# A graph-network stack on one core: a seam piece one slot later, the last round's normalisation behind the relu, clearing and small loads in other slots

## What is computed

```python
x = layernorm(x + prelu(adj @ (x @ W0) + b0))            # layer 0
x = layernorm(x + adj @ (x @ W1) + b1)                   # layer 1
h = x                                                    # layer 2: five rounds of a gated unit
for l in range(5):
    m = A.T @ (h @ Wg[l])            # A = (adj != 0)
    r = sigmoid(m @ Wir + h @ Whr); z = sigmoid(m @ Wiz + h @ Whz)
    n = tanh(m @ Win + r * (h @ Whn)); h = (1 - z) * n + z * h      # biases left out
x = layernorm(x + h * mask)
for g, idx in enumerate(GROUPS):                         # layer 3: only nodes 0..24, five node groups
    a = D^-1/2 (adj[idx][:, idx] + I) D^-1/2
    fused[idx] += w[g] * relu(a @ relu(a @ x[idx] @ W1g + b1g) @ W2g + b2g)
x = layernorm(x + fused)
```

## Time and profile before

| what | value |
|---|---|
| median of 3 runs | 989.18 us (988.3 to 990.01) |
| the profiled execution | 988.7 us, span 986.9 us |
| PE busy | 950.6 us, 96% |
| DVE busy | 820.8 us, 83% |
| ACT busy | 770.9 us, 78% |
| POOL busy | 749.0 us, 76% |
| stage one, 0 to 163 us | PE busy 151.1 us |
| middle stage, 163 to 872 us | PE busy 705.1 of 709 us |
| closing stage, 872 to 987 us | PE busy 94.5 of 115 us |

### The profile page before, as it was taken

How to read it: one execution, slowest core, us unless ns; L and a number is a source line. 1 busy time by engine, 2 the same in 40 slices (tenths; PEclk the granted TensorE clock), 3 DMA queues, 4 the chain that set the end, 5 groups by cost and what they waited for, 6 DMA issues and landing times.

```text
span 986.9 us, 19418 instructions
## 1 busy us (share of the span) xinstructions
PE 950.6 (96%) x6010; PEld 574.5 (58%) x6010; DVE 820.8 (83%) x2077; ACT 770.9 (78%) x1324; POOL 749.0 (76%) x844
## 2 busy tenths in 40 slices
PE   7999998999999999999999999999999999989894
PEld 6999996554444544444554555554445455468783
DVE  5999998898879999988898899789879987946555
ACT  5698896888887877887887889788887977865552
POOL 4777888567989897987988798889778887974101
PEclk9999999999999999999999999999999999999997
DMA  7543450333744563375448345654943563440020
GB/s 191 132 119 108 131 129 18 63 72 65 118 75 65 102 115 81 59 133 105 81 80 154 76 66 115 115 107 89 164 88 55 108 127 67 77 91 18 26 66 28
DMA packets 295406, 90.74 MB, mean 92 GB/s; under 512 B 222514, under 2 KB 295175, under 8 KB 295303
## 3 DMA queue, kind: packets, MB, share of 16 engines
q1 hardware_dynamic: 295302, 89.49, 45.8%
HBM read 28.67 MB, written 8.81 MB: 38 GB/s over the span
## 4 chain that ended last, share of the span: by engine, by line
PE 71%; DVE 10%; POOL 6%; issue 6%; ACT 3%; DMA 2%; SPq 0%; POOLq 0%; DVEq 0%; ACTq 0%
PE psum L1560 16%; PE psum L1565 16%; PE psum L1561 16%; PE psum L1485 8%; PE psum L1592 6%; POOL shared L765 2%; PE psum L1640 2%; PE psum L1673 2%; DMA shared<-shared 1%; DVE x3q L1020 1%; PE psum L1659 1%; PE psum L1483 1%; DVE shared L1342 1%; PE psum L1518 1%; DVE shared L1349 1%
## 5 line engine op out<-in xcount | busy, mean ns | idle before, releaser
L765 POOL TENSOR_TENSOR shared<-shared 128x512 f32<-128x512 f32 x160 | 203.7, 1273 | 34.6 <-ACT shared L974 34.5
L724 POOL TENSOR_TENSOR shared<-shared 128x512 f16<-128x512 f32 x128 | 148.3, 1158 | 52.9 <-ACT shared L928 52.8
L1565 PE MATMUL psum<-shared,wx_hi 128*128 128x512 f16 x480 | 182.1, 379 | 2.0 <-DVE shared L1368 1.7
L1560 PE MATMUL psum<-shared,wh_hi 128*128 128x512 f16 x480 | 182.2, 380 | 0.5 <-DVE shared L1342 0.4
L1560 PE MATMUL psum<-shared,wx_hi 128*128 128x512 f16 x480 | 181.9, 379 | 0.0
L1561 PE MATMUL psum<-shared,wx_lo 128*128 128x512 f16 x480 | 181.9, 379 | 0.0
L1565 PE MATMUL psum<-shared,wh_hi 128*128 128x512 f16 x480 | 181.9, 379 | 0.0
L1561 PE MATMUL psum<-shared,wh_lo 128*128 128x512 f16 x480 | 181.9, 379 | 0.0
L1342 DVE SCALAR_TENSOR_TENSOR shared<-psum,bhn,shared 128x512 f32<-128x512 f32 x160 | 119.9, 749 | 52.4 <-ACT shared L945 49.9
L974 ACT ACTIVATE shared<-psum,brz,unscale 128x512 f32<-128x512 f32 x160 | 124.2, 776 | 46.2 <-PE psum L1565 46.1
L910 ACT ACTIVATE shared<-psum 128x512 f16<-128x512 f32 x160 | 95.6, 597 | 52.7 <-PE psum L1592 52.7
(11 more groups left out here) (183 smaller groups left out, 1742.8 us busy)
## 6 DMA issues: line engine op xcount, KB each, us to landing
m<-in_adj_dram SPq DMA_DIRECT2D x32, 256.0 KB, 3.0
m<-in_x_dram SPq DMA_DIRECT2D x32, 256.0 KB, 3.4
adjr<-in_adj_dram SPq DMA_DIRECT2D x32, 256.0 KB, 3.2
out_dram<-x SPq DMA_DIRECT2D x8, 768.0 KB
shared<-shared SPq DMA_TRANSPOSE x192, 3.2
out_dram<-shared SPq DMA_DIRECT2D x32, 50.0 KB
v<-in_L_gnn_W_dram SPq DMA_DIRECT2D x10, 128.0 KB, 2.4
x3q<-x SPq DMA_DIRECT2D x16, 50.0 KB
```

Of the source, the lines that this page charges most:

```text
L724: nc.gpsimd.tensor_tensor(HT_LO[s % 2], HT[s][:, :], HT_HI[s % 2], ALU.subtract).then_inc(b_htl, 1)
L765: nc.gpsimd.tensor_tensor(ZH[s % 2][:, :], ZW[s % 2][:, :], HT[s][:, :], ALU.mult).then_inc(b_zh, 1)
L1560: mm(dst, w_h[:, col:col + P], h[:, :], start=start, stop=False)
L1565: return mm(dst, w_h[:, col:col + P], lo[:, :], start=False, stop=stop)
```

## The change

**Seam.** For step 33 alone, `second_inner` moves from piece 1 to piece 2 and `transposed_y1` from piece 2 to piece 3, one slot later each.

**Closing stage.** `support_out(0)` goes to slot 162, ahead of the last tanh. HID, TT and TN get other addresses, so HID's first relu waits for the last state (`b_h`) where it waited for `b_fl`, and the copies wait for `b_fl`. `rest(k)` stands behind the relu of its step on ACT and DVE; on POOL it stays where it was. Its slots are no longer six a step but from 4, 10, 16, 18, 20 to 22.

**Clearing, loads and scaling.** Other slots for five of the sixteen clearings (45, 46, 65, 66 and 110 become 39, 59, 69, 79 and 99); small loads only in slots with t mod 20 outside 2 to 5; the last scaling of groups 3 and 4 in two slots.

Step sizes become a list, `IN_STEP`, which holds eight times sixteen as before; slices over graphs are written with its entry and come out the same.

In the places of tensors and the slots of `rest`:

```diff
-    REST = 6
+    REST_FROM = (4, 10, 16, 18, 20, LAST_LAG)
...
-        HID = [part([P, CS]) for c in range(HC)]
         TT = part([P, CS])
         TN = part([P, PAIRS * P])
+        assert used[0] <= RT_AT
+        used[0] = RT_AT
+        HID = [part([P, CS]) for c in range(HC)]
...
-                first = TURN + 4 + k * REST
-                for j in range(first, min(first + REST, TURN + LAST_LAG)):
+                for j in range(TURN + REST_FROM[min(k, 5)], TURN + REST_FROM[min(k + 1, 5)]):
```

On ACT:

```diff
-                if part == 2 and has(3):
+                if part == (3 if k == ALONE else 2) and has(3):
                     transposed_y1(k)
...
+                if t == ITEMS + 2:
+                    support_out(0)
...
-                    if gth(x) == GROUPS - 1:
-                        support_out(0)
...
+                if has(0):
+                    n = IN_STEP[k]
+                    act.wait_ge(c_h[0], k + 1)
+                    if k == 0:
+                        act.wait_ge(b_h, ITEMS)
...
+                    last.then_inc(c_rh[0], 1)
                 if k >= 1:
                     rest(k - 1)
...
                 if has(0):
-                    act.wait_ge(c_h[0], k + 1)
+                    n = IN_STEP[k]
+                    act.wait_ge(c_t, k + 1)
                     if k == 0:
                         act.wait_ge(b_fl, GROUPS)
```

On DVE:

```diff
-                if i in (17, 18, 19):
-                    for g in ((1,), (2,), (3, 4))[i - 17]:
+                if i in (17, 18, 19, 20):
+                    for g in ((1,), (2,), (3,), (4,))[i - 17]:
...
                 if has(3):
                     apply_q(k - 3)
-                if k >= 1:
-                    rest(k - 1)
...
                     last.then_inc(c_rh[1], 1)
+                if k >= 1:
+                    rest(k - 1)
```

On PE, and the tables of slots:

```diff
-                if part == 1 and has(3):
+                if part == (2 if k == ALONE else 1) and has(3):
                     second_inner(k)
...
-L3_DEG, L3_AN = 6, 21
-L3_AT = (3, 4, 8, 9, 13, 14, 32, 33, 44, 45, 46, 47, 48, 49, 52, 53, 64, 65, 66, 67)
+L3_DEG, L3_AN = 6, 22
+L3_AT = (3, 4, 8, 9, 13, 14, 32, 33, 44, 45, 46, 47, 48, 49, 52, 53, 64, 65, 66, 67, 68)
...
-ZERO_AT = (31, 45, 46, 50, 51, 65, 66, 70, 71, 85, 86, 90, 91, 105, 106, 110)
-M2_LOAD, M2_PER = 76, 1
+ZERO_AT = (31, 39, 50, 51, 59, 69, 70, 71, 79, 85, 86, 90, 91, 99, 105, 106)
+FREE_OF_STORES = [t for t in range(76, 160) if t % 20 not in (2, 3, 4, 5)]
+M2_AT = FREE_OF_STORES[:4 * sum(len(r) for r in RUNS)]
+N2_AT = FREE_OF_STORES[len(M2_AT):len(M2_AT) + 4 * NG]
...
-N2_LOAD, N2_PER = 118, 1
```

More of the change, by code:

```diff
@@ L58, in graph_stack_kernel @@
     BY_ACT = STEPS_A - 2
-    REST = 6
+    REST_FROM = (4, 10, 16, 18, 20, LAST_LAG)
     GC = 16
-    STEPS_C = B // GC
+    IN_STEP = [GC] * (B // GC)
+    FROM = [sum(IN_STEP[:k]) for k in range(len(IN_STEP))]
+    STEPS_C = len(IN_STEP)
     PAIRS = GC // 2
@@ L988, in step_c @@
                 if k >= 1:
                     rest(k - 1)
+                if has(1):
+                    n = IN_STEP[k - 1]
+                    act.wait_ge(c_o, k)
+                    ov = OT[:, :].rearrange("p (b s c) -> p b s c", b=2, c=NODES)[:, 0:by_bank(n), :, :]
+                    oa = OA[:, :].rearrange("p (b s c) -> p b s c", b=2, c=ADDED)[:, 0:by_bank(n), :, :]
+                    for g in range(NG):
+                        c = OFFS[g] - NODES
+                        nc.scalar.activation(oa[:, :, :, c:c + SIZES[g]] if g else ov, slots2(2, g, n), ACT.Relu,
+                                             bias=nwb2[:, g:g + 1], scale=nw[:, g:g + 1]).then_inc(c_ro, 1)
@@ L990, in step_c @@
                 if has(0):
-                    act.wait_ge(c_h[0], k + 1)
+                    n = IN_STEP[k]
+                    act.wait_ge(c_t, k + 1)
                     if k == 0:
                         act.wait_ge(b_fl, GROUPS)
-                    for g in range(NG):
-                        last = nc.scalar.activation(grp(HID[0], g), by_group(0, g), ACT.Relu,
-                                                    bias=b1T[:, g * HC:g * HC + 1])
-                    last.then_inc(c_rh[0], 1)
@@ L1006, in step_c @@
-                if has(0):
-                    act.wait_ge(c_t, k + 1)
                     for g in TT_ON_ACT:
-                        last = nc.scalar.activation(slots(TT[:, :], g), per_graph(by_group(4, g), g), ACT.Copy)
+                        last = nc.scalar.activation(slots(TT[:, :], g, n), per_graph(by_group(4, g, n), g), ACT.Copy)
                     last.then_inc(c_tt, 1)
@@ L1382, in apply_q @@
                 wait_apart(dve, c_rsq, k + 1)
-                for i in range(QUADS):
+                for i in range(IN_STEP[k] // G4):
                     last = nc.vector.tensor_scalar(xq[0:QN, i * D:(i + 1) * D], xq[0:QN, i * D:(i + 1) * D],
@@ L1425, in step_c @@
                     wait_apart(dve, c_bsq, k - 1)
-                    for i in range(QUADS):
+                    for i in range(IN_STEP[k - 2] // G4):
                         last = nc.vector.bn_aggr(MVQ[0:QN, 2 * i:2 * i + 2], STQ[0:QN, 6 * i:6 * i + 6])
@@ L1632, in step_c @@
                     pe.wait_ge(c_tts, k)
-                    for i in range(PAIRS):
+                    for i in range(IN_STEP[k - 1] // 2):
                         last = nc.tensor.transpose(psum[0:W2, 6 * 512 + i * P:6 * 512 + (i + 1) * P],
```

124 lines of the change are left out of this document (64 added, 60 removed).

## The result

The changed kernel takes 984.59 us (median of 6 runs, 984.18 to 985.43). The kernel before, run beside it, takes 989.63 (6 runs, 988.3 to 993.12). The ratio is 0.9943, with a 95% interval of 0.9924 to 0.9962. The profiled execution took 984.47 us around a span of 982.4, against 988.7 around 986.9. So it is 4.2 us faster from profile to profile (4.5 by the spans), 5.0 by the medians and 5.6 by the ratio, whose interval goes from 3.8 to 7.5 us. The forecast was 981.3, in a range of 978.5 to 985.5; the narrower band of 979.8 to 982.8, which it gave 60%, was missed.

A forecast was written before the change was run, and what follows sets the result against it. PE is busy 96% of the span, so gains come only where it stands: 1.34 + 0.90 + 1.82 + 0.94 + 2.43 = 7.4 us off the profiled 988.7 gives 981.3 us, range 978.5 to 985.5.

The forecast's parts named there:

- Rival 1: Closing stage, steps 2 and 3: the clock drops in PE's new waits, 1.4 us twice, so 984.1 us; chance 8%.
- seam: Start of the middle stage: PE's 2.60 us wait for POOL is filled until item 2's transpose lands; 1.34 us gained.
- pair in slots 67 and 68: Middle stage: two 36-element DVE operations go into two slots instead of both into slot 67; 0.9 us gained.
- stores, slots 86, 106, 126: Middle stage: without small loads around each store, the transposes behind the stores land in time; 1.8 us gained.
- clearings, slots 42, 62, 82, 102: Middle stage: five of sixteen clearings change slots, counted at nothing, 0.3 us either way.
- start of the closing stage: Support's evacuation ahead of the last tanh: PE leaves its wait sooner and the first relu starts earlier; 0.94 us gained.
- its steps: Closing stage, steps 1 to 5: 4.33 us excess of step 3 goes, 0.95 us comes back in steps 2 and 3; 2.43 gained.
- Rival 2: Stores: the small load is not what slows the transpose, so 1.3 to 1.8 us stay, about 983.0 us; chance 12%.
- rival 4: Slots 108 to 117: weight loads and small loads meet, transposes land late, 13.6 us over ten slots, 995 us; chance 3%.

## Why the prediction was partly right

Its time was 3.3 us too low, its range held the time, and its sign was right. That the range held it is in part luck: its upper end was there for the rivals, and none of them is what happened. Rival 1 had even named 984.1 us. But the clock stood at 1.00 from 884 to 944 us, and the two steps took the 12.51 us of the main forecast; the time alone would have pointed to the wrong cause. Term by term, against the profile of before:

| term | forecast, us | measured, us |
|---|---|---|
| seam | 1.34 | 1.27 |
| pair in slots 67 and 68 | 0.90 | 0.94 |
| stores, slots 86, 106, 126 | 1.82 | 1.50 |
| clearings, slots 42, 62, 82, 102 | 0 (0.3 either way) | -2.83 |
| start of the closing stage | 0.94 | 0.90 |
| its steps | 2.43 | 2.51 |
| all else | 0 | -0.1 |
| sum | 7.4 | 4.2 |

**The step that failed** is one sentence: "Five of the sixteen clearings change slots, three of them out of slots next to DVE's scalings; I count that at nothing, with 0.3 us either way." It looked at where the clearings left, not at what they came to stand before. The row was in the trace: POOL's gap of 0.34 us ahead of L735, for an operation of 0.81, and DVE's L1323 0.07 us ahead of it. Leaving slots 45, 46, 65 and 66 gave nothing: slots 46 and 66 stayed at 4.60 and 4.54 (4.58 and 4.53 before). The bound of 0.3 had no row under it. With -2.83 us in its place (of which slot 82's 0.42 is uncertain) the forecast would have been 984.1, against 984.47 in the profile and 984.59 by the median.

**The seam, the pair and the start** held with their mechanisms: item 2 was held by its transpose, one 36-element operation a slot costs 0.18 us, and L1006 is no longer released by POOL. The prediction's reading that the tiny operations wait for a turn is borne out: in the kernel after each takes 1.13 us (from 454.06 and from 458.57) and ends 0.05 us after POOL's L733, which began 0.08 us ahead of it.

**The stores** were mis-sized by 0.3. The transpose behind the store in slot 86 still took 4.9 us to land with the small load gone, and 3.9 in slot 106:

```profile
DMA to landing us min/median/max: 4.9/4.9/4.9
...
DMA to landing us min/median/max: 3.9/3.9/3.9
```

In eight other kernels with the loads moved slot 86 took 4.33 to 4.97 us, so up to 0.6 stays there with the store alone ahead of the transpose. Rival 2 was right in part. In slot 86 the row of the prediction held: 4.9 us is 0.26 over the 4.64 that are free, and the slot is 0.28 longer than 4.33. Of rival 4 (weight loads and small loads meet) nothing came: slots 110 to 118 are at 4.33 to 4.35.

**The closing steps** were right in sum, and each of the two waits was 1.1 us, inside the ends given. But the 4.33 us of excess that the sum starts from hold the fall of the clock, 1.5 to 1.7 us, which came in only two of five executions. Averaged over the profiles the steps are worth 1.5 us, 0.9 less than forecast, and the seam 2.2, 0.9 more. That the two terms cancel is luck. Rival 1, the clock falling in the new waits, was not seen in any of the six profiles that have them. But the argument against it was wrong: the 2.60 us wait brought the clock down in three of five executions, and the 1.72 us wait in one.

With these averages the places sum to 4.4 us (2.2 + 0.9 + 1.7 - 2.8 + 2.4), so they do not account for the 5.0 by the medians against 4.2 by the profiles; the interval of 3.8 to 7.5 holds both. The first profile of the kernel before was one of its better executions: 988.7, where its medians in four sets of runs are 989.6 to 990.4. The changed kernel has none of the waits of 2.60, 2.80 and 1.72 us, and its six runs lie within 1.3 us of each other; those of the kernel before beside it within 4.8.

## What to carry to other kernels

A small operation moved to an engine with idle time overall needs a gap of its own size where it lands. If there is none, see what it pushes, and what that then meets on the engine that shares a port with it. Ask the windows by slot, not the page's share (POOL is 76% busy in the span and 95% in those slots). And take two or three profiles of the kernel before when PE has long waits in it: behind the same wait the clock fell in some executions and not in others, so a term read from one of them may be a throw of a coin.

## What the runs showed of the hardware

- A POOL clearing of 0.81 us lengthens DVE's float32 scalings in SBUF (L1331) from 0.66 to 1.23 us, although it reads nothing. Next to POOL's L744 of 1.20 us a scaling of 0.41 takes 1.37, and next to L774 of 1.27 and a clearing of 0.80 right behind it a pair of 0.60 takes 1.75. Whichever began first went first: DVE when it was 0.07 us ahead, POOL when it was 0.11 us ahead.
- Behind the same wait of 2.80 us the granted clock fell in two of five executions, behind 2.60 us in three of five, and in one of five it fell behind the wait of 1.72 us at the start of the closing stage. A fall cost 1.5 to 1.8 us, that last one 0.7.
- In the kernel after, a transpose right behind a store, with no small load beside it, landed in 3.9 to 4.9 us in slots 106 and 86; with a small load in the kernel before it took 4.8 and 6.0.
